# The second batch's gate and up products in seven block products instead of eight

## What is computed

```python
x = x + _layernorm(_L0_attn_ref(_layernorm(x, axis=-1), Wq, Wk, Wv, Wo), axis=-1)
# feed-forward: x (2,1024,512), w_gate and w_up (512,2048), w_down (2048,512)
n = _layernorm(x, axis=-1)
h = silu(n @ w_gate) * (n @ w_up)
h_sparse = of every 4 neighbours of h the 2 of largest size, the rest 0
x = x + _layernorm(h_sparse @ w_down, axis=-1)
```

## Time and profile before

| | |
|---|---|
| median of three runs | 1196.28 us |
| span of the profiled execution | 1194.3 us |
| its own time | not listed apart from the three runs; they are 1.4 to 2.5 us above its span |
| PE busy | 1183.0 us, 99% |
| DVE, ACT, POOL busy | 64%, 42%, 41% |
| DMA | 95.03 MB, mean 80 GB/s |
| chain that ended last | PE 95%, DVE 3% |

### The profile page before, as it was taken

One profiled execution on the slowest core, in us unless ns is written; L12 is line 12 of the kernel. 1 busy time (PEld: TensorE's weight loads), 2 busy tenths in 40 slices (PEclk: granted clock), 3 DMA queues, 4 the chain that ended last, 5 costly groups with the idle time before them and its releaser, 6 DMA issues.

```text
span 1194.3 us, 16009 instructions
## 1 busy us (share of the span) xinstructions
PE 1183.0 (99%) x5958; PEld 998.5 (84%) x5958; DVE 762.5 (64%) x1300; ACT 497.5 (42%) x981; POOL 493.6 (41%) x399
## 2 busy tenths in 40 slices
PE   9999999999999999999999999999999999999997
PEld 7888888888888888888888888888888888888885
DVE  8944756756664456666665476676567765555568
ACT  5534444544544345455355443433333342333322
POOL 6421533515555125244245444443425552334313
PEclk9999999999999999999999999999999999999998
DMA  7221323323534214133143222211103231212111
GB/s 225 80 78 52 102 72 80 89 49 80 146 98 141 58 47 131 47 87 94 30 124 102 97 80 71 71 62 45 62 12 105 97 98 45 62 44 62 45 44 71
DMA packets 58222, 95.03 MB, mean 80 GB/s; under 512 B 6944, under 2 KB 15392, under 8 KB 58144
## 3 DMA queue, kind: packets, MB, share of 16 engines
q1 hardware_dynamic: 58144, 94.01, 27.2%
HBM read 67.24 MB, written 11.53 MB: 66 GB/s over the span
## 4 chain that ended last, share of the span: by engine, by line
PE 95%; DVE 3%; DMA 0%; issue 0%; POOL 0%; ACT 0%; SPq 0%; DVEq 0%
PE bank_q L567 10%; PE bank_q L565 10%; PE bank_q L566 10%; PE bank_y L567 5%; PE bank_y L566 5%; PE bank_y L565 5%; PE bank_od L724 5%; PE bank_od L565 4%; PE bank_od L566 4%; PE bank_od L567 4%; PE bank_od L727 4%; PE bank_t L567 4%; PE bank_t L565 4%; PE bank_t L566 4%; PE bank_s L565 4%; PE bank_s L566 4%
## 5 line engine op out<-in xcount | busy, mean ns | idle before, releaser
L565 PE MATMUL bank_q<-x_hi,w_hi 128*128 128x512 f32 x432 | 172.9, 400 | 0.0
L1339 POOL TENSOR_TENSOR w_lo<-stage,w_hi 128x512 fp32r<-128x512 f32 x80 | 109.3, 1376 | 147.9 <-ACT w_hi L891 147.2
L567 PE MATMUL bank_q<-x_lo,w_hi 128*128 128x512 f32 x432 | 168.9, 391 | 0.0
L566 PE MATMUL bank_q<-x_hi,w_lo 128*128 128x512 f32 x432 | 168.3, 390 | 0.0
L1339 POOL TENSOR_TENSOR big_lo<-hidden,big_hi 128x512 fp32r<-128x512 f32 x30 | 69.0, 2321 | 188.5 <-ACT big_hi L1006 188.5
L1339 POOL TENSOR_TENSOR big_lo<-q_rows,big_hi 128x1024 fp32r<-128x1024 f32 x31 | 74.0, 2386 | 117.2 <-ACT big_hi L930 117.2
L997 ACT ACTIVATE scratch<-hidden 128x512 f32<-128x512 f32 x64 | 40.6, 634 | 176.2 <-DVE hidden L1255 176.2
L567 PE MATMUL bank_y<-wout_lo,a_hi 128*128 128x512 f32 x256 | 100.0, 391 | 0.0
L565 PE MATMUL bank_y<-wout_hi,a_hi 128*128 128x512 f32 x256 | 99.8, 390 | 0.0
L566 PE MATMUL bank_y<-wout_hi,a_lo 128*128 128x512 f32 x256 | 99.8, 390 | 0.0
L567 PEld LDWEIGHTS bank_q<-x_lo,w_hi 128*128 128x128 f32 x432 | 81.1, 188 | 17.6
(11 more groups left out here) (333 smaller groups left out, 2987.3 us busy)
## 6 DMA issues: line engine op xcount, KB each, us to landing
q_rows<-scratch SPq DMA_DIRECT2D x116, 128.0 KB, 2.3
x_rows<-x SPq DMA_DIRECT2D x48, 256.0 KB, 2.9
stage<-wq SPq DMA_DIRECT2D x32, 256.0 KB, 2.7
stage<-wo SPq DMA_DIRECT2D x32, 256.0 KB, 2.7
stage<-wg SPq DMA_DIRECT2D x32, 256.0 KB, 2.6
stage<-wu SPq DMA_DIRECT2D x32, 256.0 KB, 2.8
stage<-wd SPq DMA_DIRECT2D x32, 256.0 KB, 2.6
x<-x_rows SPq DMA_DIRECT2D x16, 256.0 KB, 2.4
```

The costliest lines, as they stand in the source:

```text
L565: pe.matmul(ps, whi, xhi, start=first, stop=False, skip_group_check=True)
L566: pe.matmul(ps, wlo, xhi, start=False, stop=False, skip_group_check=True)
L567: return pe.matmul(ps, whi, xlo, start=False, stop=last, skip_group_check=True)
L1339: return pool.tensor_tensor(dst, full, hi.bitcast(F32), ALU.subtract)
```

## The change

Batch 0's feed-forward slots (0 to 31) compute as before. Batch 1's slots 32 to 63 become eight quads k of four beats. A quad makes gate and up of 256 hidden rows for all 1024 tokens. Feature halves, hidden halves and token halves form a two by two block product, made by seven block products in Winograd's form of Strassen's scheme, with the sums of x taken in advance (`combine_x`: T1 to T4 from the four blocks B of x, ten DVE operations of 128x1024 in slots 28 to 31, cast by ACT and subtracted by POOL in slots 30 to 33). A block product (`product`) is 6 matmuls of 128x512. Four banks hold the running sums: gX, uX (bank_q), gY (bank_t), uY (bank_st). Beat 0 makes four products, beat 1 four, beat 2 two and beat 3 four. Between them ACT copies gX and uX out (`keep_sums`), DVE adds gY and uY to the copies (`gate_sum`, `up_sum`), ACT takes the silu and DVE multiplies (`gated`).

Of the seven units of weights of a quad and side, four are sums of weight blocks. They are made in slots 0 to 20 in 16 rounds: SP loads two pieces (512 KB), DVE makes four sums of 128x256 (`sum_weights`), ACT casts and POOL subtracts 128x1024 each, and SP stores high and low parts (1 MB) to the DRAM tensor `s_keep`; in the quads they come back split, 512 KB a unit, into a ring of five. The other units (0, 1 and 6 of seven) are loaded raw and split by ACT and POOL in the quads (`split_unit`). All of batch 1's down weights are split by POOL.

Batch 1's down products are placed anew (`down_beat`): beats 32 to 37 have one each (the last of batch 0), 38 to 42 none, 43 to 48 one each, 49 two, 50 none, 51 to 56 one each, 57 two, 58 none, 59 to 62 one each, 63 none; twelve come after beat 63. `MID_1`, the slots in which batch 1's x is turned, moves from 8..22 to 13..26. Buffers are laid over others that are free by then.

The diff, cut to what is spoken of here:

```diff
-def down_at(n):
-    y = n - 6 if n < 60 else 54 if n == 61 else n - 9 if n >= SLOTS else -1
-    return y if 0 <= y < SLOTS else None
+def down_beat(y):
+    if y < EDGE:
+        return y + 6
+    if y >= LAST:
+        return y + 9
+    return SLOTS if y > 51 else 8 * (y // 8) + 11 + min(y % 8, 6)
+
+
+def add_beat(y):
+    n = down_beat(y)
+    return n if n >= SLOTS or n < EDGE else n + 1
...
+SUM_AT = [0, 1, 2, 3, 5, 6, 7, 9, 10, 11, 13, 14, 16, 17, 19, 20]
...
+DOWN_AT = {NU: (35, 36, 37, 41), NU + 1: (42, 43, 44, 45), NU + 2: (52, 53, 54, 55), NU + 3: (60, 61, 62, 63)}
...
-MID_1 = [8, 10, 12, 14, 16, 18, 20, 22]
+MID_1 = [13, 15, 17, 19, 22, 24, 25, 26]
...
+            def load_unit(v):
+                k, j = v // 7, v % 7
+                i = v % RING
+                if v < RING:
+                    g.wait_ge(pe_u if v == 4 else pe_g, EDGE - 3 + v % 4)
...
+                    g.wait_ge(pe_ux if side == "u" else pe_gx, count)
+                if j < 2:
+                    for half in HALVES:
+                        sp.dma_start(ring_lo[:, i, half], (wu if j else wg)[k // 2, 2 * (k % 2)][:, half]
+                                     ).then_inc(ld_r[i], 16)
+                elif j < 6:
+                    sums_kept(g, 2)
+                    sums_kept(g, 3)
+                    sp.dma_start(w_hi[:, i, :].bitcast(F32), s_keep[2 * k + j % 2, 0, j // 4]).then_inc(ld_r[i], 16)
+                    sp.dma_start(w_lo[:, i, :].bitcast(F32), s_keep[2 * k + j % 2, 1, j // 4]).then_inc(ld_r[i], 16)
+                else:
+                    for up in range(2):
+                        sp.dma_start(ring_lo[:, i, HALVES[up]], (wu if up else wg)[k // 2, 2 * (k % 2) + 1][:, HALVES[1]]
+                                     ).then_inc(ld_r[i], 16)
+
+            def load_down(u, i):
...
+            def product(ps, v, side, of, first):
+                wh, wl = w_hi[:, v % RING, HALVES[side]], w_lo[:, v % RING, HALVES[side]]
+                for kk in range(2):
+                    c = slice(kk * P, kk * P + P)
+                    ins = three(ps, wh[:, c], wl[:, c], of[0][:, kk, :], of[1][:, kk, :], first and kk == 0, kk == 1)
+                return ins
...
+                v = 7 * k
+                g.wait_ge(pool_t, 3)
+                unit_wait(v + 2)
+                g.wait_ge(act_n, 6 * k + 1)
+                product(gX, v + 2, 0, T2, False).then_inc(pe_gx, 1)
+                g.wait_ge(dve_cg, 3 * k + 1)
+                product(gY, v + 2, 1, T3, True)
+                unit_wait(v + 3)
+                g.wait_ge(act_n, 6 * k + 2)
+                product(uX, v + 3, 0, T2, False).then_inc(pe_ux, 1)
+                g.wait_ge(dve_cu, 3 * k + 1)
+                product(uY, v + 3, 1, T3, True)
+
+            def products_5(k):
+                v = 7 * k
+                unit_wait(v + 4)
+                g.wait_ge(act_n, 6 * k + 3)
+                product(gX, v + 4, 1, T1, False).then_inc(pe_gx, 1)
+                unit_wait(v + 5)
+                g.wait_ge(act_n, 6 * k + 4)
+                product(uX, v + 5, 1, T1, False).then_inc(pe_ux, 1)
+
+            def products_34(k):
+                v = 7 * k
+                g.wait_ge(act_n, 6 * k + 5)
+                product(gX, v + 4, 0, B22, False).then_inc(pe_gx, 1)
+                g.wait_ge(dve_cg, 3 * k + 2)
+                g.wait_ge(pool_t, 4)
+                unit_wait(v + 6)
+                product(gY, v + 6, 0, T4, False).then_inc(pe_gx, 1)
+                g.wait_ge(act_n, 6 * k + 6)
+                product(uX, v + 5, 0, B22, False).then_inc(pe_ux, 1)
+                g.wait_ge(dve_cu, 3 * k + 2)
+                product(uY, v + 6, 1, T4, False).then_inc(pe_ux, 1)
...
+            def split_unit(v):
+                i = v % RING
+                g.wait_ge(ld_r[i], 32 * turns_of(v))
+                copy(w_hi[:, i, :], ring_lo[:, i, :]).then_inc(act_r, 1)
+
...
+            def silu(k, i):
+                if i == 2:
+                    g.wait_ge(pe_gx, 6 * k + 5)
+                    g.wait_ge(dve_hx, 4 * k + 1)
+                    act.activation(gates[0], gX, ACT.Silu).then_inc(act_s, 1)
+                else:
+                    g.wait_ge(dve_cg, 3 * k + (1, 2, 0, 3)[i])
+                    act.activation(gates[(0, 1, 0, 2)[i]], gates[(0, 1, 0, 2)[i]], ACT.Silu).then_inc(act_s, 1)
+
+            def keep_sums(k, i):
+                u, h = NU + k // 2, i // 2
+                row = 2 * (k % 2) + (i > 0)
+                g.wait_ge(pe_gx, 6 * k + (1, 3, 4)[i])
+                g.wait_ge(dve_hx, 4 * k - (1, 0, 2)[i])
+                g.wait_ge(pe_at, SLOTS)
+                g.wait_ge(pe_pv, SLOTS)
+                copy(gates[(0, 2, 1)[i]], gX).then_inc(act_n, 1)
+                hid1_free(g, u, row, h)
+                g.wait_ge(pe_ux, 6 * k + (1, 3, 4)[i])
+                copy(hid1(u, row, h), uX).then_inc(act_n, 1)
+
...
+                    if beat == 0:
+                        if not late and v:
+                            absolute(v - 1, 1, 0)
+                        if k:
+                            keep_sums(k, 0)
+                        silu(k, 0)
+                        if late:
+                            absolute(v, 0, 1)
+                    if beat == 1:
+                        keep_sums(k, 1)
+                        if v:
+                            split_hidden(2 * (NU + v - 1) + late)
+                        if n == EDGE + 1:
+                            cast_t(3)
+                    if beat == 2:
+                        keep_sums(k, 2)
+                        silu(k, 1)
+                        split_unit(7 * k + 6)
+                        if late:
+                            absolute(v, 0, 0)
+                        elif v:
+                            absolute(v - 1, 1, 1)
+                    if beat == 3:
+                        silu(k, 2)
+                        silu(k, 3)
+                        if k + 1 < QUADS:
+                            split_unit(7 * k + 7)
+                            split_unit(7 * k + 8)
+                if n == SLOTS:
+                    absolute(NU - 1, 1, 0)
+                    split_hidden(STEPS - 2)
+                if n == SLOTS + 1:
+                    absolute(NU - 1, 1, 1)
+                if n == SLOTS + 2:
...
+            def combine_x(step):
+                high = [block[0].bitcast(F32) for block in (B11, B21, B12, B22)]
...
+                    g.wait_ge(dve_wl, NU)
+                g.wait_ge(dve_t, (0, 0, 1, 2, 3, 4, 5, 7, 8, 9)[step])
+                to, first, other, op = ((raw_t1, high[b12], high[b11], ALU.subtract),
+                                        (raw_t3, high[b22], high[b12], ALU.subtract),
...
+            def gate_sum(k, i):
+                to = gates[i]
+                g.wait_ge(act_n, 6 * k + (1, 5, 3)[i])
+                g.wait_ge(pe_gx, 6 * k + (2, 4, 6)[i])
+                dve.tensor_tensor(to, to, gY, ALU.add).then_inc(dve_cg, 1)
+
+            def up_sum(k, i):
+                to = hid1(NU + k // 2, 2 * (k % 2) + (i > 0), i % 2)
+                g.wait_ge(act_n, 6 * k + (2, 6, 4)[i])
+                g.wait_ge(pe_ux, 6 * k + (2, 4, 6)[i])
+                dve.tensor_tensor(to, to, uY, ALU.add).then_inc(dve_cu, 1)
+
+            def gated(k, i):
+                u, row = NU + k // 2, 2 * (k % 2)
+                g.wait_ge(act_s, 4 * k + i + 1)
+                if i == 2:
+                    hid1_free(g, u, row, 1)
+                    g.wait_ge(pe_ux, 6 * k + 5)
+                    dve.tensor_tensor(hid1(u, row, 1), uX, gates[0], ALU.mult).then_inc(dve_hx, 1)
+                else:
+                    to = hid1(u, row + (i > 0), i % 2 if i < 2 else 0)
+                    g.wait_ge(dve_cu, 3 * k + (1, 2, 0, 3)[i])
+                    dve.tensor_tensor(to, to, gates[(0, 1, 0, 2)[i]], ALU.mult).then_inc(dve_hx, 1)
...
+                if EDGE <= n < SLOTS:
+                    k, beat = quad_of(n)
+                    v, late = k // 2, k % 2
+                    if beat == 0:
+                        if v and not late:
+                            pair_1(v - 1, 1, 0)
+                        elif v:
+                            keep_masks(v - 1, 1)
+                        if k:
...
+                            keep_masks(v - 1, 0)
+                    if beat == 1:
+                        gated(k, 0)
+                        for y in downs:
+                            add_down(y)
+                        if v:
+                            keep_rows(v - 1, late)
+                            hidden_lows(v - 1, late)
+                        if late:
+                            pair_1(v, 0, 1)
+                    if beat == 2:
+                        gate_sum(k, 1)
+                        for y in downs:
+                            add_down(y)
+                        up_sum(k, 1)
+                        if late:
+                            pair_1(v, 0, 0)
+                    if beat == 3:
+                        gated(k, 1)
```

(30 more changed lines are left out.)

463 lines of the change are left out of this document (401 added, 62 removed).

## The result

The change makes the kernel slower: 1244.26 us, the median of four runs (1239.95 to 1246.39), for 1196.33 (1195.75 to 1196.78) before, a ratio of 1.0398 (95%: 1.0379 to 1.0417). I had forecast 1199.3 and a range up to 1210. The profiled execution took 1244.21 us, with a span of 1242.4. Without any new wait the span would have been 1194.3 - 21.8 = 1172.5. So 69.9 us of waits and lost clock have to be explained, and I had forecast 24.8.

What follows compares the result with a forecast made beforehand. PE, busy 99% of the span, was taken as the bound. From 1196.3 us, 21.8 removed and 24.8 of waits added (3.3 + 6.0 + 0.4 + 2.5 + 5.0 + 7.6) gave 1199.3 us, range 1187 to 1210.

Steps and rivals of the forecast that it cites:

- Removed: Batch 1's quads: 672 matmuls stand for 768, so 96 of 0.227 us, 21.8 us, come off PE.
- The fourth rival: Block products of 6 matmuls go slower than 12, so the saving fails; near 1210 us, chance 0.02.
- Slots 0 to 31: The rounds' 26 us of DVE additions, ACT casts and POOL low parts cost PE 0, bounds 0 and 3.
- asked for two slots ahead: Slots 0 to 31, SP: loads behind 1 MB stores land after 2.6 us, asked for two slots ahead; taken 0.
- The edge: Slots 28 to 32: ten DVE operations delay bank_t; 0.3 us, plus three meetings with POOL at 1.0: 3.3 us.
- Unit 6: Beat 3 without a down product: gY waits for unit 6's low part, 2.0 us each in quads 1, 4, 6.
- Quad 1's beat 3: No down product there; PE waits for the next quad's first unit: 2.5 us, bounds 1 and 3.5.
- Quad 2: One down product, at its end; ranking lengthens DVE's chain and PE waits there: 5.0 us, bounds 4 and 7.
- The end: After the last quad, twelve down products wait for two groups ranked in turn: 7.6 us, bounds 7 and 8.5.
- The third rival: PE's clock falls in the waits; three falls of 6 us each add 9: 1208 us, chance 0.08.
- my sign: What would show the third rival: a granted clock in the quads under 0.95.
- The second rival: DVE and POOL meet everywhere: ten more meetings and the edge at 7 give 1213 us, half 1206; chance 0.20.

Runs made afterwards that it cites:

- e1: The changed kernel with all 16 rounds of weight sums in slots 0 to 31 left out: 1221.75 us.
- e3: The changed kernel with only POOL's low part of every round left out, the raw sum stored in its place: 1219.98 us.
- e9: The changed kernel with SP asking for each round's stores a slot later, and its stores and loads behind the slot's other loads: 1282.99 us.
- e8: The changed kernel with six of the ten DVE sums of x at the edge left out: 1238.07 us.
- e11: The changed kernel with the last two of DVE's ten sums of x (T4's) moved behind slot 32's work: 1244.72 us.
- e10: The changed kernel with ACT casting unit 6 ahead of the copies of gX and uX and the silu in beat 2: 1237.10 us.
- e14: The changed kernel with the edits of e10 and e11, T2's low part not waiting for T4's sums, and units' loads ahead of rows' stores: 1228.00 us.
- e4: The changed kernel with idle matmuls added ahead of six waits of PE in the second batch's part: 1238.29 us.

## Why the prediction was wrong

**Removed, 21.8 us: held.** PE's matmuls follow each other in the quads at 0.227 us, and quads 3 and 5 took 30.3 and 30.6 us for the 30 forecast. The fourth rival, that the change doesn't save what it says, is refuted.

**Slots 0 to 31, 0 forecast with bounds 0 and 3: 27.0 measured. This is the step that failed.** All my upper bounds together give 1217, so without this term no choice among the others reaches 1244. The step took DVE's idle two fifths as cover for 26 us of additions priced at their length when alone. My own price of a subtraction beside POOL, 1.70 for 0.69, stands in the very next paragraph and was applied only at the edge. The additions took 56.2 us, the other work grew by another 11, and the 161 of e1 and these 67 make 228, which no longer keep up in 241. e1 to e3 show that it takes both halves: without rounds, or without either half of the meeting, these slots take 2 to 3 us more than before (what makes these 2 to 3 was not tried). In the change PE stood 17.0 us there (268 less 250.99 busy) and ran 6.8 us' worth at the lower clock. My "asked for two slots ahead" was wrong too: a round's load waits for the store that empties its buffer, and e9 shows what that chain costs when it gets longer. How much of the 27 us the 9.9 us of DVE's waits for loads make by themselves wasn't tried.

**The edge, 3.3 forecast: 5.8, and 3.4 at the lower clock.** The place and the cause were right (e8, e11). I counted three meetings at 1.0. The timeline of DVE after has four, and they cost 1.6, 1.1, 0.7 and 1.0 more than the 0.69 and 1.22 of the same work alone:

```profile
928.66 2.31 DVE L1608 TENSOR_TENSOR scratch<-scratch 128x512 bf16<-128x512 f32 x1
930.89 1.78 DVE L1609 TENSOR_TENSOR scratch<-scratch 128x512 f32<-128x512 f32 x1
...
934.92 1.91 DVE L1672 TENSOR_TENSOR stage<-x_hi,stage 128x1024 f32<-128x1024 f32 x1
936.87 2.17 DVE L1672 TENSOR_TENSOR stage<-stage,x_lo 128x1024 f32<-128x1024 f32 x1
```

**Unit 6, 2.0 each in quads 1, 4 and 6: 1.95, 2.00 and 2.00.** Right, and e10 removes them. The other quads had 0.2 to 0.3.

**Quad 1's beat 3, 2.5: 1.7. Quad 2, 5.0: 6.0, but not in one wait:** 1.4 for a unit from DRAM, 1.2 for ACT's copy and 3.5 for unit 6's low part, and none at its end, where I had put the 5.0. e10 took unit 6's wait away, and even then PE doesn't wait for quad 3's first unit; what grows is the wait at quad 2's first unit, to 4.6 for the 2.5 that I had. **Quad 0, nothing forecast: 3.5** for a unit from DRAM, asked for only at 958.8 behind a store for which SP waited; e14's order removed it.

**The end, 7.6: 9.7,** of which 1.7 is the clock.

**The third rival, 9 us at 0.08, came true beside everything else.** It put three falls; there are ten places worth up to 20.5 us. From 933 to 1192 the granted clock is 0.95, at the bound that I had named and not under it, so my sign was set too low. My sum priced the waits but put what stands behind them at nothing. The trace now has the row for the return that I missed: 0.58 and 0.53 over 4 and 7 us of work. **The second rival** was the right mechanism in the wrong place: I put it at the edge and in the quads and gave 0.20 to up to 14 us more; it works where the rounds are. Its sign, DVE's sums over 2 us each in slots 28 to 31, was met by one of ten.

Together: 27.0 in slots 0 to 31, 23.9 of waits at the edge and in the quads for the 17.2 forecast, 11.9 of clock there, 9.7 at the end: 72.5 for 69.9 measured, since not each slow stretch costs its full 1.7 us (e4).

That "slower" was the likeliest of my three outcomes, at 0.50, is no merit of the sum: it was added up from an edge, quads and an end that came out near their prices, and the larger part of the loss lay elsewhere. Two of my figures don't follow from the working: the lower bounds give 18.4 only with 1.3 for the edge, which has no bound there, and four down products from 15.4 on end at 26.3 and not at 25.6. Neither enters the 1199.3.

## What to carry to other kernels

Work that is put under cover is priced at what it takes beside the work already there, and the cover is measured on the engine that it lands on, stretch by stretch: here 26 us of additions became 56, and two pieces of added work that were each free cost 24 us together. A wait of PE of some 2 to 3 us can cost 1.7 us again at the lower clock, though not each does, so a saving that is paid for with several short waits is worth less than the waits say. And in a ring of buffers that goes through several in-order queues, moving one link later moves all: 39 us in e9.

## What the runs showed of the hardware

A DVE subtraction of 128x512 beside POOL's of 128x1024 lasted to the end of POOL's, 2.86 us for 0.69; that was more than I had expected.

The low clock came after waits of PE as short as 1.95 us (996.6 to 998.8 in the change). Waits of 1.74, 1.73 and 1.81 us in the same execution left it at 1.00, but so did one of 1.94 us (698.3 to 700.4) and the one of 3.3 us at 800. In e4 the same place at 800, with a shorter wait, was followed by the low clock. So these traces give no length of wait that decides it. The Trainium skill ("TensorE: Matmul & The Clock Gate", "What's actually happening") says that the array falls to half rate when idle and comes back after sustained work; the trace agrees with both: around slot 22 it has 1.00 before the wait, 0.58 behind it and, after some 3 us of PE's work, 0.96 in the window that follows.
